# Summing squares for the root mean square of two state-space mixers: on VectorE over a strided view, or in column-tiled products

## The reference

```
x = x + mixer_a(layernorm(x))      # 16 heads of 64, state 64
x = x + ffn(layernorm(x))
x = x + mixer_b(layernorm(x))      # 64 heads of 16, state 128
x = x + ffn(layernorm(x))
```

```
mixer_a:  yf = y * silu(gate);  var = mean(yf * yf);  yn = norm_w * (yf * rsqrt(var + eps));  yn @ out_proj.T
mixer_b:  var = mean(y * y);    yn = y * rsqrt(var + eps) * norm_w;  (yn * silu(z)) @ out_proj
```

## Time and profile before

| | |
|---|---|
| median of three runs | 2862.99 us |
| span of the profiled execution, first to last instruction | 2859.7 us |
| TensorE busy | 2733.3 us (96%) |
| VectorE busy | 2009.9 us (70%) |
| ScalarE busy | 1527.0 us (53%) |
| GpSimd busy | 926.1 us (32%) |

### The profile page before, as it was taken

The page is one execution under the profiler, slowest core; times in us unless marked ns, Lnnn a source line. Parts: engine busy times, 40 slices in busy tenths (PEclk is TensorE's granted clock), DMA queues, the critical chain, the costliest instruction groups (busy, mean ns, idle before and its releaser), DMA issues. The chain is left out here.

```text
span 2859.7 us, 49906 instructions
## 1 busy us (share of the span) xinstructions
PE 2733.3 (96%) x17464; PEld 1845.0 (65%) x17464; DVE 2009.9 (70%) x3695; ACT 1527.0 (53%) x2418; POOL 926.1 (32%) x614
## 2 busy tenths in 40 slices
PE   7999999999999999996899999999999999997996
PEld 6777766777766665455666666666666666664453
DVE  5666666666666663377788888888888888885267
ACT  3444444445455442341577666766667776665242
POOL 2222223222223321232233444333333334332134
PEclk9999999999999999998999999999999999998998
DMA  4000000000000034145000000000000000022333
GB/s 125 23 23 22 22 22 22 23 28 29 22 22 22 16 121 152 45 147 204 12 23 22 22 22 16 21 22 22 15 15 22 22 22 22 15 95 89 112 118 133
DMA packets 79935, 139.59 MB, mean 49 GB/s; under 512 B 17896, under 2 KB 17896, under 8 KB 78832
## 3 DMA queue, kind: packets, MB, share of 16 engines
q1 hardware_dynamic: 70752, 125.92, 12.9%
q10 hardware_dynamic: 9104, 12.63, 1.4%
HBM read 104.98 MB, written 33.55 MB: 48 GB/s over the span
## 5 line engine op out<-in xcount | busy, mean ns | idle before, releaser
L655 PE MATMUL work<-b_xnT,shared_w 128*128 128x256 f32 x2304 | 545.8, 388 | 1.8 <-DVE b_parts L1192 1.3
L655 PE MATMUL work<-a_xnT,shared_w 128*128 128x256 f32 x2176 | 509.4, 392 | 1.3
L655 PEld LDWEIGHTS work<-b_xnT,shared_w 128*128 128x128 f32 x2304 | 426.1, 191 | 90.6 <-issue 30.1
L655 PEld LDWEIGHTS work<-a_xnT,shared_w 128*128 128x128 f32 x2176 | 419.0, 195 | 73.8 <-issue 12.3
L1232 DVE TENSOR_TENSOR b_decay<-b_decay,b_gt 128x1024 f32<-128x1024 f32 x256 | 351.7, 1395 | 119.3 <-ACT b_decay L943 115.8
L936 ACT ACTIVATE b_decay<-seg 128x1024 f32<-128x1024 f32 x256 | 248.5, 1029 | 112.0 <-PE seg L781 111.8
L943 ACT ACTIVATE b_decay<-b_decay 128x1024 f32<-128x1024 f32 x256 | 266.1, 1073 | 0.0
L1406 POOL TENSOR_TENSOR b_rhs<-b_l_side,of_head 128x1024 fp32r<-128x1024 f32 x32 | 82.0, 2563 | 552.4 <-DVE b_l_side L1201 552.4
L1441 POOL TENSOR_TENSOR a_y<-a_y,a_skip 128x1024 f32<-128x1024 f32 x32 | 90.9, 2840 | 484.1 <-DVE a_y L1221 484.1
L1111 DVE SCALAR_TENSOR_TENSOR shared_cv<-shared_pre,a_conv_w,shared_cv 128x256 f32<-128x256 f32 x432 | 189.7, 482 | 74.6 <-ACT shared_cv L880 68.9
L1111 DVE SCALAR_TENSOR_TENSOR shared_cv<-shared_pre,b_conv_w,shared_cv 128x256 f32<-128x256 f32 x480 | 232.1, 517 | 14.2 <-ACT shared_cv L880 6.3
(11 more groups left out here) (314 smaller groups left out, 4612.4 us busy)
## 6 DMA issues: line engine op xcount, KB each, us to landing
shared_x<-in_L_attn_a_x SPq DMA_DIRECT2D x16, 512.0 KB, 3.5
a_x_res<-in_L_attn_a_x SPq DMA_DIRECT2D x32, 256.0 KB, 2.6
x_mid<-a_x_res SPq DMA_DIRECT2D x32, 256.0 KB, 2.1
shared_w<-in_L_ffn_d_w SPq DMA_DIRECT2D x2, 4096.0 KB, 14.0
f_d_w<-in_L_ffn_d_w SPq DMA_DIRECT2D x2, 4096.0 KB, 14.5
f_x_res<-x_mid SPq DMA_DIRECT2D x8, 1024.0 KB, 5.9
f_bc_w<-x_mid SPq DMA_DIRECT2D x8, 1024.0 KB, 5.6
shared_x<-x_mid SPq DMA_DIRECT2D x16, 512.0 KB, 3.6
```

The lines of the kernel that those rows point to most:

```text
L655: mm = nc.tensor.matmul(dst, w_in[:, k, col:col + m], xnT[:, k, :], start=(k == 0), stop=(k == KD - 1))
```

## The change

The eight column-tiled products of each tile (`rs0` and `prs`) and their place in the list of steps go, and the column `quad_row` with them. VectorE's `square_sums` no longer copies from PSUM: it waits for ScalarE's squares and reduces `sq` itself, over a view in which the eight blocks are innermost (each output is the sum of 8 elements that lie 128 elements apart), into the same `rs` of 128 x 128. The turning product stays, now against a column of ones.

```
-            nc.vector.tensor_reduce(c["quad_row"][:], c["ident"][:].rearrange("p (q e) -> p e q", e=32)[:, 0:1, :],
-                                    mybir.AxisListType.X, ALU.add).then_inc(built, 1)
...
-                    + (["prs"] if prev else []) + ["yoff0a", "yoff0b", "seg0.0"] + (["prt"] if prev else [])
+                    + ["yoff0a", "yoff0b", "seg0.0"] + (["prt"] if prev else [])
...
-            steps += ["rs0", "yoff1a", "yoff1b", "seg1.0", "rt0", "out0"]
+            steps += ["yoff1a", "yoff1b", "seg1.0", "rt0", "out0"]
...
-        epi_steps = ["prs", "prt", "pout"]
+        epi_steps = ["prt", "pout"]
...
-                    elif name in ("rs0", "prs"):
-
-                        pe.wait_ge(sq_done, FREE + 2 * (2 * i + (name == "rs0")))
-                        for b in range(KE):
-                            q = b % 4
-                            mm = nc.tensor.matmul(bank[32 * q:32 * q + 32, 0:P], ones[:, 0:32], sq[:, b, :],
-                                                  start=(b < 4), stop=(b >= 4))
                     elif name in ("rt0", "prt"):
                         pe.wait_ge(rs_ready, FREE + 2 * i + (name == "rt0"))
-                        mm = nc.tensor.matmul(bank[:, 0:1], rs[:], c["quad_row"][:], start=True, stop=True)
+                        mm = nc.tensor.matmul(bank[:, 0:1], rs[:], ones[:, 0:1], start=True, stop=True)
...
-                def square_sums(sec, name):
-                    dve.wait_ge(work_full, sec.full(name))
-                    nc.vector.tensor_copy(rs[:], sec.bank(name)[:, 0:P]).then_inc(rs_ready, 1)
+                def square_sums(tile):
+
+                    dve.wait_ge(sq_done, FREE + 2 * tile + 2)
+                    nc.vector.tensor_reduce(rs[:], sq[:].rearrange("p b t -> p t b"), mybir.AxisListType.X, ALU.add
+                                            ).then_inc(rs_ready, 1)
```

More of the change, by code:

```diff
@@ L216, in build_constants @@
     c["keep"] = sb("keep", [P, NSUP + 1])
-    c["quad_row"] = sb("quad_row", [P, 1])
     hd = sb("hd", [P, 2, 4, 16])
@@ L285, in _ @@
                                     ).then_inc(built, 1)
-            nc.vector.tensor_reduce(c["quad_row"][:], c["ident"][:].rearrange("p (q e) -> p e q", e=32)[:, 0:1, :],
-                                    mybir.AxisListType.X, ALU.add).then_inc(built, 1)
-            dve.wait_ge(built, 4)
+            dve.wait_ge(built, 3)
             nc.vector.tensor_scalar(c["sign_row"][:], c["low_row"][:], -2.0, 1.0, ALU.mult, ALU.add).then_inc(built, 1)
             nc.vector.tensor_scalar(c["s_row"][:], c["l_row"][:], -1.0, 1.0, ALU.mult, ALU.add).then_inc(built, 1)
-            dve.wait_ge(built, 6)
-            count = [6]
+            dve.wait_ge(built, 5)
+            count = [5]
             def link(ins):
@@ L573, in freed @@
                 eng.wait_ge(state_ready, FREE + i * 4 + 2 * int(name[5]) + (2 if FOLD else "ab".index(name[6]) + 1))
-            elif name in ("rs0", "prs"):
-                eng.wait_ge(rs_ready, FREE + i * 2 + (name == "rs0"))
             elif name in ("rt0", "prt"):
@@ L1292, in supertile @@
                     if prev:
-                        square_sums(sec, "prs")
+                        square_sums(2 * i - 1)
                     from_state(sec, 0)
@@ L1325, in supertile @@
                         gate(sec, 0)
-                    square_sums(sec, "rs0")
+                    square_sums(2 * i)
                     from_state(sec, 1)
@@ L1394, in _ @@
                 sec = epilogue()
-                square_sums(sec, "prs")
+                square_sums(2 * NSUP - 1)
                 rms_var(sec, "prt")
```

## The result

The changed kernel takes 2914.50 us (median of 4 runs, 2913.65 to 2915.99) against 2863.17 us before (2861.88 to 2865.03): a ratio of 1.0179 [1.0165, 1.0194]. The forecast was 2921 us, the range 2857 to 2936. The profiled span went from 2859.7 to 2913.5 us, +53.8.

A forecast was written before the change was run, and what follows sets the result against it. It took nearly always busy TensorE to bound both mixers, with waits costing one for one. The terms summed to 64R - 88.8, at R = 2.29 +57.8 us on 2862.99, so 2921 us; range 2857 to 2936 us.

The forecast's parts named there:

- The path: At all four places, TensorE's next step follows the second `from_state`: 0.06 us ahead of `out0`, 0.13 us ahead of `xnT0`.
- R: Time of VectorE's new reduction: forecast 2.29 us, from 0.143 us fixed plus 1024 elements at 0.0021 us.
- B's middle: Start of `out0` in Mixer B, 16 times: change of R - 0.90 us, forecast +1.39 us each.
- B's beginning: Start of `xnT0` in Mixer B, 15 times: change of R - 0.89 us, forecast +1.40 us each.
- A's middle: Start of `out0` in Mixer A, 16 times: change of R - 2.22 us, forecast +0.07 us each.
- A's beginning: Start of `xnT0` in Mixer A, 15 times: change of R - 1.57 us, forecast +0.72 us each.
- The floor of -0.64 us: Limit set on the gain at A's middle: never below -0.64 us, what TensorE itself saves from the deleted products.
- Whatever makes it wait costs time one for one: TensorE has next to no idle time in either mixer, so each wait lengthens the kernel by its own length.
- The formula: Sum over both mixers' middles, beginnings and epilogues: 64R - 88.8 us for R of 1.58 and more.
- The first: Rival: the reduction's stride costs nothing, R = 1.22 us, -4.9 us, so 2858 us; chance 0.29.
- The second: Rival: R below 1.58 us and VectorE works off its lateness in B; 2843 or 2822 us; chance 0.10.
- The third: Rival: the stride costs three steps, R up to 3.25 us, +119 us, so 2982 us; chance 0.08.

The follow-up runs named there:

- The run with the wait filled: Changed kernel, with seven unused 128x128 identity products on TensorE in Mixer B where it would wait for `from_state`; 2881.10 us, 1.0063 of the kernel before.
- adjacent elements: Changed kernel, with the reduction grouping 8 neighbouring elements instead of 8 lying 128 apart (wrong sums); 2836.95 us, 0.9912 of the kernel before.
- VectorE's new order: Changed kernel, in Mixer B only: reduction behind `from_state` in the middle, ahead of the first `make_xdt` at the beginning; 2829.98 us, 0.9880 of the kernel before.
- the step of two: Changed kernel, with the reduction's 8 elements 2 apart (8 bytes) instead of 128 apart, grouping the wrong elements; 2840.76 us in one run.
- the last run above: VectorE's new order, with the reduction and `from_state` ahead of `make_xdt` in Mixer A too; 2850.20 us, 0.9946 of the kernel before.

## Why the prediction was right, and where it was wrong

**The path: right.** In all four places TensorE's next step follows the end of the second `from_state`, and `from_state` follows the reduction. With the measured R the terms fit: B's middle +1.01 predicted, +1.00 measured; B's beginning +1.02 and +1.04; A's middle -0.31 and -0.44; A's beginning +0.34 and +0.19. The idle time that the row of waits shows in B, 1.7 us, is this delay and the 0.64 us of products that TensorE no longer has: 1.02 + 0.64 = 1.66. The prediction's "some 1.4 us each in B" left that part out, in the row though not in the sum. The slope of 2.0 us of B's supertile for each us of R, shown over three values of R, is the firmest support. The floor of -0.64 us does not hold in B: without a reduction a supertile fell by 1.55 us.

**R: the step that was mis-sized.** "It is nearer to two ... so I take two steps: R = 2.29 us" failed. The reading of `quad_row` was 6 to 8 ns for 4 elements, so 1.5 to 2.0 ns each; with 1.75 the same sum is 0.143 + 1024 x 0.00175 = 1.93 us, and 1.91 was measured. I rounded to a whole number of steps for which no row spoke. That is 64 x (2.29 - 1.91) = 24 us too much. Of the two pages of the Trainium skill weighed there, Advanced Engine Details and Errata (section SBUF Cachelines) was right that a stride is penalised (0.70 of the 1.91 us here). The statement of the Trainium skill in VectorE: DVE Perf Modes, section on the 1x mode, that this mode assumes nothing about strides and yields one result a cycle holds here for steps of 4 and 8 bytes (1.21 us) and not for 16 and more (1.91 us and over).

**"Whatever makes it wait costs time one for one": the step that failed.** The delay in B cost 1.0 us in itself and, in 20 of 32 tiles, 1.3 to 1.7 more (2.8 in the epilogue), since the product behind it ran partly at half the granted clock: +34.1 us, which no term had. The run with the wait filled shows it apart from the delay. The granted clock stood in the earlier trace rows, and I priced no change of it.

**The sum.** The formula at R = 1.91 gives 64 x 1.91 - 88.8 = +33.4 us, of it +32.4 in B and +1.0 in A. With the clock term B comes to +66.5 us; measured are +60.2. Of the 6 us between them 2 are in the steady supertiles, which give 16 x (80.53 - 78.64) = 30.2 in the place of 32.4; the other 4 lie at the end of the mixer: from the output product in the middle of supertile 13 to that of supertile 15 the changed kernel takes 148.8 us against 146.0, so 2.8 more, where two bodies of the loop lose 7.8. Why the end loses less is open. A came out at -6.7, by the two places -0.44 x 16 + 0.19 x 15 = -4.2; the stretches of lower clock fell there from 9 to 7, at which 20.5 us were lost before and 17.1 after, and that is about the rest. From the forecast: 57.8 - 24 for R, + 34 for the clock, - 8 in A and - 6 in B is +54, against +53.8. So the near hit is luck: a reduction taken too dear stood against a clock term left out.

**The rivals.** The first, a stride that costs nothing, fell: 1.91 us. With R at 1.21, tried by itself, its time was also wrong: 2837 and not 2858 us, since A loses its slow stretches as well. The second (VectorE works its lateness off) fell: the reduction in B waited for the squares for only 1.3 us in all, and not more with adjacent elements, where R is below 1.58 as this rival asks. The third fell with R. Its upper end was no pace of VectorE: the 1623 ns of the earlier trace rows are a mean over products beside GpSimd's and others, and in VectorE's new order two of them take 1.30 us. What would have shown the forecast wrong in its mechanism, R over 2 us and B not 30 us longer, did not come about. But the sum at the measured R did not give the time either, so it was not wrong in size alone.

**Open.** Why TensorE's clock falls is not settled. By the size of the wait the runs show this much, in B's stage from 1500 to 2500 us: with adjacent elements TensorE waits 25 times for `from_state`, up to 1.0 us, and the clock stays at 1.00; with the step of two, 25 times up to 1.2 us, and it falls once; behind the 27 waits of 1.7 us of the changed kernel (1500 to 2600 us) it falls 15 times. In the supertile shown, the wait at the middle is followed by a slow output product, and the one at the beginning, of 1.75 us, is followed by one at 7.03 us. And in Mixer A it falls without such a wait: in the kernel before, from 195 to 207 us, TensorE is busy for 11.85 of 12 us, and from 203.4 us its granted clock is 0.50 for 3.4 us. So the filled wait settles it for the changed kernel's Mixer B alone.

## What to carry to other kernels

Ask of each instruction that is made longer what stands behind it on its engine: with the same reduction of 1.9 us right ahead of `from_state` the kernel lost 51 us; with it moved in Mixer B, behind `from_state` in the middle and ahead of `make_xdt` at the beginning, it gained 34. A wait on a TensorE that was busy is priced with what its clock does afterwards, so look at the granted clock around the waits in small windows before calling a wait one for one. A measured time for each element is not to be rounded to whole steps.

## What the runs showed of the hardware

- VectorE's reduction of 1024 float32 to 128: 1.21 to 1.22 us at steps of 4 and 8 bytes, 1.97 to 1.99 at 16, 1.91 to 1.92 at 512.
- ScalarE writing 512 float32 over a step of 32 bytes: 1133 to 1139 ns, against 601 to 626 over adjacent ones.
- After 1.71 us of idle time TensorE ran some 3.4 us of its next output product at a granted clock of 0.50 (1.2 GHz), and 20 of Mixer B's 32 output products were longer; with the idle time filled the clock stayed at 1.00 and none was. In Mixer A of the kernel before it fell to 0.50 from 203.4 us with TensorE busy for 11.85 of the 12 us around.
- A product of VectorE with two operands in SBUF beside a GpSimd product: in the last run above GpSimd began at 528.49 and ended at 530.85, and VectorE's first product began at 528.55 and took 3.38 us, the second 1.21. Less the 2.30 us up to GpSimd's end, 1.08 is left of the first, a little under its usual 1.22: VectorE looks blocked until GpSimd's instruction is over. The Trainium skill (SBUF — State Buffer, section Who interferes with whom) calls the port that the two share an exclusive lock, and the trace agrees.
